# Attention's scores as single f32 products on row tiles instead of exact bf16 parts stacked through DRAM

## The reference

```python
xs = xn.reshape(B, C, H * W).transpose(0, 2, 1)
qkv = (xs @ w_proj.T + b_proj).reshape(B, H * W, N_HEADS, 3 * D_K)
q, k, v = jnp.split(qkv, 3, axis=-1)
attn = jnp.einsum('bihk,bjhk->bijh', q, k) * D_K ** 0.5
attn = jax.nn.softmax(attn, axis=2)
h = jnp.einsum('bjhk,bijh->bihk', v, attn)
h = h.reshape(B, H * W, N_HEADS * D_K) @ w_out.T + b_out
h = h * jax.nn.sigmoid(h) + xs
```

## Time and profile before

| | |
|---|---|
| median of three runs | 1559.66 us |
| profiled execution | 1557.11 us |
| its span, first to last instruction | 1555.3 us |
| mean granted TensorE clock | 0.969 |
| busy: PE (TensorE), DVE, ACT, POOL | 1428.2, 1250.3, 1064.4, 390.5 us |
| DMA queue of the program's transfers | 109.44 MB, 42.2% of 16 engines |

### The profile page before, as it was taken

How to read it: one execution, slowest core, us unless ns; L and a number is a source line. 1 busy time by engine, 2 the same in 40 slices (tenths; PEclk the granted TensorE clock), 3 DMA queues, 4 the chain that set the end, 5 groups by cost and what they waited for, 6 DMA issues and landing times.

```text
span 1555.3 us, 52670 instructions
## 1 busy us (share of the span) xinstructions
PE 1428.2 (92%) x22818; PEld 769.5 (49%) x22818; DVE 1250.3 (80%) x2641; ACT 1064.4 (68%) x1484; POOL 390.5 (25%) x268
## 2 busy tenths in 40 slices
PE   3799999998996999999999999999999999999996
PEld 2456455555882344455455444454544445455442
DVE  7977777788779888879888788888888878888852
ACT  2344566664660388777777777777777777777786
POOL 0600011112141031432514315134051340513111
PEclk9999999999995699999999999999999999999998
DMA  9000666662042125436354372543825527255322
GB/s 224 6 2 13 98 106 108 108 108 37 1 105 68 38 26 97 79 53 125 25 110 69 63 126 27 108 92 40 127 27 107 96 37 128 33 100 103 33 21 28
DMA packets 59264, 112.81 MB, mean 73 GB/s; under 512 B 20600, under 2 KB 45432, under 8 KB 58904
## 3 DMA queue, kind: packets, MB, share of 16 engines
q1 hardware_dynamic: 59032, 109.44, 42.2%
HBM read 54.22 MB, written 26.10 MB: 52 GB/s over the span
## 4 chain that ended last, share of the span: by engine, by line
PE 57%; DVE 17%; DMA 10%; SPq 6%; ACT 6%; issue 3%; POOL 0%; ACTq 0%; DVEq 0%
PE ps L1058 25%; PE ps L1135 11%; DVE arena L1522 8%; PE ps L969 6%; DMA arena<-arena 5%; PE ps L941 5%; PE ps L986 4%; SPq L399 3%; ACT arena L859 3%; ACT arena L724 3%; DMA k_dram<-arena 2%; PE ps L1031 2%; SPq L394 2%; DVE bn L1247 2%; PE ps L1115 2%
## 5 line engine op out<-in xcount | busy, mean ns | idle before, releaser
L1522 DVE TENSOR_REDUCE arena<-ps 128x1 f32<-128x392 f32 x1600 | 804.7, 556 | 148.9 <-PE ps L1058 148.2
L859 ACT ACTIVATE arena<-ps 112x784 f32<-112x784 f32 x896 | 700.7, 825 | 179.3 <-PE ps L1058 174.5
L1058 PE MATMUL ps<-arena 112*32 112x392 bf16 (+2 forms) x13312 | 706.1, 335 | 34.2 <-ACT arena L859 17.2
L1058 PEld LDWEIGHTS ps<-arena 112*32 112x32 bf16 (+2 forms) x13312 | 343.7, 95 | 453.7 <-DVE arena L1522 143.1
L1135 PE MATMUL ps<-arena 112*32 112x392 f32 x3584 | 376.5, 492 | 1.2 <-issue 0.9
L612 POOL TENSOR_TENSOR arena<-arena 128x784 f32<-128x784 f32 x31 | 58.0, 1871 | 566.8 <-DMA arena<-arena 566.8
L724 ACT ACTIVATE arena<-ps,magic,arena 128x784 f32<-128x784 f32 x128 | 128.2, 1004 | 47.0 <-PE ps L969 47.0
L969 PE MATMUL ps<-arena 96*128 96x392 f16 x768 | 141.7, 334 | 9.2 <-DMA arena<-arena 3.6
L1135 PEld LDWEIGHTS ps<-arena 112*32 112x32 f32 x3584 | 110.9, 110 | 41.4 <-issue 2.2
L969 PEld LDWEIGHTS ps<-arena 96*128 96x128 f16 x768 | 67.9, 98 | 82.0 <-ACT arena L724 22.6
L941 PE MATMUL ps<-arena 64*64 64x392 f32 x1152 | 104.6, 505 | 3.2 <-ACT arena L674 3.2
(11 more groups left out here) (123 smaller groups left out, 1049.1 us busy)
## 6 DMA issues: line engine op xcount, KB each, us to landing
arena<-arena SPq DMA_DIRECT2D x256, 84.2 KB, 2.8
arena<-q_dram SPq DMA_DIRECT2D x64, 294.0 KB, 4.8
arena<-k_dram SPq DMA_DIRECT2D x64, 294.0 KB, 4.6
q_dram<-arena SPq DMA_DIRECT2D x48, 196.0 KB, 6.7
k_dram<-arena SPq DMA_DIRECT2D x48, 196.0 KB, 4.1
x<-x_in SPq DMA_DIRECT2D x8, 784.0 KB, 21.2
out<-x SPq DMA_DIRECT2D x16, 392.0 KB, 5.5
arena<-arena SPq DMA_DIRECT2D x124, 49.0 KB, 5.7
```

The source lines that it names most:

```text
L859: nc.scalar.activation(probs[w % 2][:, 2 * pair:2 * pair + 2, :], two(2 * place, rows=slice(0, TT)), ACT.Exp).then_inc(s_taken, 1)
L1058: last = nc.tensor.matmul(to[at:end, :], stationary[:, at:end], moving, start=start, stop=stop, tile_position=(0, at))
L1522: nc.vector.tensor_reduce(mx[img % 2][:, c, v:v + 1], scores, AX.X, ALU.max).then_inc(s_mf, 1)
```

## The change

What it does, part by part:

- q and k are made for each image (`has_qk`, U_Q, U_K = 3, 5), with the four heads' 16 channels at partitions 0, 32, 64 and 96. ACT writes them as f32 from PSUM into the tiles that the scores use. The splits, the tiles of parts, the DRAM tensors, stores and stacks are gone. Row 16 of each head holds minus the maximum in q and 1 in k.
- `scores`: one f32 product per head, 17 rows, 112 columns, at row tile 32 h. `max_chunk`: one f32 product per chunk, 16 rows, 128 columns, for one head; the two chunks of a unit are the two heads of the pair that the unit's scores don't use (`max_contents`). Both chunks stand ahead of the weighing. One unit an image holds the rest (the last 16 queries of each head).
- `max_t` takes one of the three banks; the DVE negates from it (ACT's copy goes), and the maxima go through DRAM in f32.
- Tokens (normalised x) of later pairs are made on POOL, ahead of time. "v" is at unit 7, "out" in odd steps at unit 23. Attention's second normalisation is prepared in two halves instead of three groups.
- Third layer: two of the first products (PRODUCTS) instead of five; the other five of FIRST run among the first maxima (`unit_product`).
- Second layer: the convolution's 128 columns as two tiles of 64 side by side; scales in two f16 parts instead of three bf16 ones (32 products instead of 48), spread over units 3 to 7 of the next pair; the shifted images are double-buffered; the normalisation runs further ahead.
- First layer: for pairs 2 to 7 ACT scales all four experts and POOL adds them; the second layer's weights are prepared by the DVE in steps 8 to 11.

```diff
-        NO_MAX = 0, 4, 22
+        NO_MAX = 0, 5, 22
 ...
         def has_qk(s):
-            return s % 2 == 1 and (s + 3) // 2 < NP
+            return s + 3 < B
 ...
         def has_out(s):
-            return s % 2 == 0 and s >= 2
+            return s % 2 == 1 and s >= 3
 ...
-        U_Q, U_K, U_V, U_OUT = 2, 4, 4, 22
+        U_Q, U_K, U_V, U_OUT = 3, 5, 7, 23
 ...
-        PRODUCTS = {10: "q", 11: "k", 12: "v", 14: "q", 15: "k"}
+        PRODUCTS = {13: "q", 14: "k"}
+        UNIT_PRODUCTS = {2: 2, 4: 3, 6: 4, 12: 5, 14: 6}
 ...
+        POOL_MIXES = range(2, 8)
 ...
+            def free_bank(n):
+                if n >= MAX_BANKS:
+                    pe.wait_ge(s_mf, n + 1 - MAX_BANKS)
+                return BANK_MAX + n % MAX_BANKS
+
+            def max_chunk(m, c):
+                img, v = divmod(m, NM)
+                bank = free_bank(nth_chunk(m, c))
                 q, k = qs[img % 4], ks[img % 4]
-                if v < NM - 1:
-                    h, it = divmod(v, QT)
-                    last = columns(ps[:, bank, 0:CH], 128, q[0:ROWS_L, h, it * 128:(it + 1) * 128],
-                                   k[0:ROWS_L, h, c * CH:(c + 1) * CH])
+                if MAX_CONTENTS[v][0] == "heads":
+                    _, pair, it, half = MAX_CONTENTS[v]
+                    at = 2 * DK * (2 * pair + c)
+                    last = nc.tensor.matmul(ps[:, bank, 0:CH], q[at:at + DK, it * 128:(it + 1) * 128],
+                                            k[at:at + DK, half * CH:(half + 1) * CH], start=True, stop=True,
+                                            tile_position=(at, 0))
 ...
-            def max_t(place):
-                nc.tensor.transpose(ps[0:NM, 2 * place, 0:128], mx_all[:, :], P("ident")).then_inc(s_s, 1)
+            def max_t(img):
+                bank = free_bank(nth_t(img))
+                pe.wait_ge(s_mx, img + 1)
+                nc.tensor.transpose(ps[0:NM, bank, 0:128], mx_all[:, :], P("ident")).then_inc(s_m, 1)
 ...
                     h = 2 * pair + j
-                    last = columns(ps[:, 2 * place + j, 0:CH], TT, ks[s % 4][0:ROWS_ALL, h, jt * TT:(jt + 1) * TT],
-                                   qs[s % 4][0:ROWS_ALL, h, c * CH:(c + 1) * CH])
+                    at = 2 * DK * h
+                    last = nc.tensor.matmul(ps[0:TT, 2 * place + j, 0:CH],
+                                            ks[s % 4][at:at + DK + 1, jt * TT:(jt + 1) * TT],
+                                            qs[s % 4][at:at + DK + 1, c * CH:(c + 1) * CH], start=True, stop=True,
+                                            tile_position=(at, 0))
 ...
-                        max_chunk(img, v, j, m, 0, after_short=(s == 0))
-                        second = lambda: max_chunk(img, v, j, m, 1, after_short=(s == 0))
+                        max_unit(max_units(s, u))
                     weigh_now(u)
-                    if after is None:
-                        second()
-                    else:
-                        extra(after, second)
+                    if after is not None:
+                        extra(after)
+                    if u == U_MT and s + 1 < B:
+                        max_t(s + 1)
 ...
-                            sp.dma_start(shifted[im][k * 3 * GC:(k + 1) * 3 * GC, g, 0:FLAT],
-                                         over).then_inc(s_shift[im], 16)
+                            sp.dma_start(shifted[p % 2][im][k * 3 * GC:(k + 1) * 3 * GC, g, 0:FLAT],
+                                         over).then_inc(s_shift[p % 2][im], 16)
 ...
+                        for at in (0, C):
+                            last = nc.tensor.matmul(ps[at:at + C, 2 * (u % 2) + c, 0:CH], w1[:, g, y, at:at + C],
+                                                    rhs, start=(y == 0), stop=(y == 2), tile_position=(0, at))
 ...
+            SUM_STEPS = 4 * NG
+            SUM_AT = {3: (0, 3), 4: (3, 6), 5: (6, 9), 6: (9, 12), 7: (12, SUM_STEPS)}
```

More of the change, by code:

```diff
@@ L304, in ring, with max_contents, max_column @@
                     yield "out"
-                if u == U_MT and s + 1 < B:
-                    yield "mt"
-        FIRST = ["q", "k", "v", "q", "k", "mt"]
+        FIRST = ["q", "k", "q", "k", "v", "q", "k"]
+        EARLY = 0, 0, 1, 1, 0, 2, 2
+        def max_contents():
+            u_of = {(nth_max(u) + AHEAD) % NM: u for u in range(NU) if u not in NO_MAX}
+            left = [[("heads", pair, it, c) for it in range(QT) for c in range(2)] for pair in range(2)]
+            found = []
+            for v in range(NM):
+                mine = left[1 - u_of[v] % 2]
+                found.append(mine.pop(0) if mine else ("rest",))
+            assert not left[0] and not left[1] and found.count(("rest",)) == 1
+            return found
+        MAX_CONTENTS = max_contents()
+        def max_column(v, k):
+            if MAX_CONTENTS[v][0] == "rest":
+                return k, NM - 1
+            _, pair, it, c = MAX_CONTENTS[v]
+            return c, (2 * pair + k) * QT + it
         def at_ring(s, what):
@@ L325, in max_units, with units_before_t, nth_chunk, nth_t @@
             return NM + AHEAD + NM * s + nth_max(u)
[L327 to L332, removed]
+        def units_before_t(img):
+            return NM + 2 if img == 0 else min(NM * B, max_units(img - 1, U_MT + 1))
+        def nth_chunk(m, c):
+            return 2 * m + c + sum(units_before_t(img) <= m for img in range(B))
+        def nth_t(img):
+            return 2 * units_before_t(img) + img
         def n_out(s):
@@ L567, in _ @@
             pool.wait_ge(s_sumx, NP)
-            for k in ks:
-                last = nc.gpsimd.memset(k[96:128, :, :], 1.0)
-            link(last)
             for a in vs:
@@ L833, in _ @@
                 l2(p)
-            take_mt(5, 1, 0)
+            for n in range(len(PRODUCTS), len(FIRST)):
+                take(n)
             def l3(s):
@@ new lines, in l1_sum @@
+            def l1_sum(p, first, end):
+                bank = 4 + 2 * (p % 2)
+                if first == 0:
+                    pe.wait_ge(s_quant, 8 * (p + 1))
+                    if p >= 2:
+                        pe.wait_ge(s_sumx, p - 1)
+                    elif p == 0:
+                        pe.wait_ge(s_added, 3 * NP)
+                for k in range(first, end):
+                    c, n = divmod(k, 2 * NG)
+                    g, half = divmod(n, 2)
+                    for im in range(2):
+                        last = nc.tensor.matmul(
+                            ps[im * C:(im + 1) * C, bank + c, 0:CH], sdiag[:, half, g, :],
+                            quant[2 * (p % 2) + im][:, g, c * CH:(c + 1) * CH],
+                            start=(n == 0), stop=(n == 2 * NG - 1), tile_position=(0, im * C))
+                if end == SUM_STEPS:
+                    last.then_inc(s_sum, 1)
```

603 lines of the change are left out of this document (262 added, 341 removed).

## The result

The changed kernel takes 2563.0 us (median), the kernel before 1559.0 in the same session: ratio 1.6424, 95% interval 1.6379 to 1.6469. Slower was forecast, but the time is 555 us above the 2008 of the prediction and outside its range (1800 to 2220). Four executions of the changed kernel took 2554 to 2600 us; the ratio leaves out the longest, a slow one. The profiled execution spans 2561.8 us, 1006.5 more than before.

A forecast was written before the change was run, and what follows sets the result against it. PE's arithmetic was taken to set the pace. 1557 + 470 (attention) + 15 (first maxima) - 24 (second layer) - 8 (first) - 5 (third) = 2005, 2008 on the runs' scale; range 1800 to 2220.

The forecast's parts named there:

- the main case: Attention: the chain as summed, 3.25 us a pair of units, +470 us in all; chance 0.72.
- rival 3: Attention: granted clock stays at 0.50, a pair takes 5.3 us, an image 80, whole about 2950; chance 0.07.
- rival 1: Attention: the bank wait is hidden, a pair takes 2.39 us, an image 37.8, whole 1718; chance 0.07.
- rival 4: Attention: row tiles don't run four at a time, image 54.6 us, whole 2213 or up to 2400; chance 0.09.
- The chain: Attention: a pair of units waits through the DVE's reduce for a bank, 3.25 us against 2.00; image 47.35 against 32.0.
- rivals 2 and 4: Rival 2, attention: switches free, fourth maximum doesn't hold the weighing, whole about 1525, chance 0.05; the other is under rival 4.
- A switch: Attention: PE going between row tiles and column tiles, twice per pair of units, costs 0.10 us each time.
- The sum that took all of the drain: Attention: if each tiling switch paid the full drain of 0.165 us, the total would be some 45 us higher.
- The first maxima: Stretch before attention: 44 us plus 4 at full clock, +35 at clock 0.50; taken as +15.
- First layer: First layer: six mixes leave the DVE for ACT and POOL, -8 us (0 to -12).
- Second layer: Second layer: fewer sum products and no tiling switches, -1.5 us for each of 16 pairs, -24 (-32 to -10).
- Third layer: Third layer: three products fewer at 1.5 us each, -5 us.

The follow-up runs named there:

- Run 1: Kernel after with scores and maxima reading 32 rows of each row tile instead of 17 and 16, added rows without effect on results: 2077.1 us.
- run 2: Kernel after with the DVE's reduce over 32 of a chunk's 392 columns and the exponent scaled by 0.05: 2047.7 us.
- run 4: Kernel after with both 32 rows in scores and maxima and the reduce over 32 of 392 columns: 1951.2 us.
- run 12: Kernel before with the change's first and second layer, POOL's second-layer subtraction waiting until the DVE has clipped the pair: 1527.8 us, ratio 0.9787.

## Why the prediction was wrong, point by point

**The step that failed** is the condition of the main case, a granted clock of 1.00 in attention, and with it the two reasons that set rival 3 at 0.07: that steady attention had run at 1.00, and that PE would stream some 85% of the time. Neither asks how many rows the new products feed. PE was busy 1983 of 2002 us and got 0.71. Run 1 shows what was missed: the same passes with 32 rows for 16 and 17 run at 1.00. The new wait has a share in it, since run 2, with a shorter one, got 0.92. Rows 13 held a warning, 0.50 with PE busy 22.27 of 24; the prediction names them under rival 3 and sets them aside by the busy share. Rival 3 was priced well (5.3 for 5.43 a pair) but put as all or nothing; the clock alternated, and the time came out between the main case and the rival. (Two rival sums are a little short: with the other terms as in rival 1, rival 3's image of 80 gives about 2980 for 2950, rival 4's 54.6 gives 2222 for 2213. Nothing hangs on it.)

**The size of it.** Run 1's span less its start of attention (the first weighing) is 2075.3 - 535.1 = 1540.2, against 1024.3 before: the chain at clock 1.00 costs +516, forecast +470. The kernel after has 2018.8 there, so the clock costs another 2018.8 - 1540.2 = 479.

**The chain** was right: 3.27 for 3.25, 2.31 for 2.3 in a pair with a unit without maxima (run 1's timeline), and run 4 shows that the reduce is in it. An image is 48.7 in run 1 (alternately 49.2 and 48.3) against 47.35; over 30 images that is 40 of the 46 missing. Rival 1 (wait hidden) falls by run 4; rivals 2 and 4 by the 3.27, which has both the switches and four row tiles at once in it.

**A switch** fits 0.10: a chain summed with it misses by 0.02 a pair. The sum that took all of the drain, 45 us more, would make the pair 3.38 and miss by 0.11 (two switches of 0.165). The lines of the first pair above show it directly: the weighing ends streaming at 1171.72 + 0.87 - 0.165 = 1172.43 and the scores start at 1172.52; the last maximum ends at 1174.14 + 0.92 - 0.165 = 1174.90 and the weighing starts at 1174.99.

**The first maxima** were put at +15 and measured +48.6. The clock was 0.50 for the whole stretch, the case priced at +35; the other 14 are in no term. A part of them is the way from the first score to the first weighing, 7.8 us (542.93 - 535.14) where it was 3.7; no run takes the rest apart.

**The earlier layers** came out right by luck, -36.6 for -37. First layer, which ends at 155.4 for 160: -4.6 for -8. Second layer, 198.9 for 216.5: -17.6 for -24, because one clip a pair is held beside POOL; 12.3 us a pair for the 11.6 of the prediction, and with the clip free 11.26 (run 12). Third layer, from 110.5 to 450.4 - 354.3 = 96.1: -14.4 for -5. What the prediction missed stands in the trace of before, in the timeline of PE at the layer's end:

```profile
475.62 3.30 PE L1031 MATMUL ps<-par,arena 112*128 112x112 f32 x14 [8.54 <-DVE x L1468]
```

PE waited 8.54 us for the DVE, whose queue held the small f32 operations of the norm's statistics for the next images; the change does them during attention. In the diff that was a changed line of step numbers, and it wasn't priced. That this wait is the whole difference is read from the two traces; no run tests it alone.

## What to carry to other kernels

Products that feed few rows of the array, with a short wait among them, can halve TensorE's clock for much of the time though the engine's record is 99% busy: look at the granted clock beside the rows and the waits, not beside the busy share, and where a row tile is half empty, widen the product with rows of zeros, which cost no time here and gave 486 us. Don't count on filler: products of 16 rows in the wait cost 219 us. Price the clock as a share of the time, not as on or off. When the mean of a group of instructions rises, look at single instructions first: one in eight had quadrupled, and moving its neighbour on POOL was worth 12 us.

## What the runs showed of the hardware that was not expected

- The granted clock rose with the rows fed, zeros included: attention at 0.71 with 16 and 17 rows, 0.97 to 0.98 with half of the added rows given in three ways, 1.00 with 32. With 16 and 17 rows and a shorter wait it was 0.92.
- Work added to keep PE busy did not raise the clock: 0.63 with three products of 16 rows, 0.70 with 32 rows, 0.71 without.
- In the kernel after, all 28 rises to 1.00 in attention came with a q, k or output product, which feeds 128 rows, or within 1.4 us of its end.
- The two levels alternated in steady, identical work: pairs of 3.27 and of 5.43 occur all through attention, in stretches (47.8 us at 0.50, then 61.5 at 1.00, in the lines above), and the mean of 0.71 is made of the two.
- A 16-bit clip on the DVE took 1.67 instead of 0.37 beside POOL's subtraction, f16 and bf16 alike, and an f32 sum in the same place took its usual 1.03.
